# A Perceiver layer with a mixture of experts: the experts' first product with the weight's blocks held in TensorE and the 128 tokens streamed

## The reference

```python
x = x + xattn(layernorm(x), ctx, bias, mask)     # 2048 context rows per batch
x = x + attn(layernorm(x))
x = x + ffn(layernorm(x), gate_w, w1, w2)

def ffn(x, gate_w, w1, w2):                       # 8 experts, hidden width 2048
    k = int(2.0 * t / 8)                          # 32 tokens per batch and expert
    probs = softmax(x @ gate_w).transpose(0, 2, 1)
    g, m = top_k(probs, k)
    xin = gather(x, m)                            # 4 x 32 = 128 tokens per expert
    h = gelu(einsum('nekd,edf->nekf', xin, w1))   # 128 x 512 by 512 x 2048
    h = einsum('nekf,efd->nekd', h, w2)           # 128 x 2048 by 2048 x 512
    return scatter_add(g[..., None] * h, m).astype(bfloat16)
```

## Time and profile before

| | us |
|---|---|
| median of 3 runs | 471.69 |
| the 3 runs | 471.41, 471.69, 473.98 |
| the profiled execution | 471.49 |
| its span in the trace | 469.8 |
| granted TensorE clock, mean over the span | 0.995 |

### The profile page before, as it was taken

The page is one execution under the profiler, slowest core; times in us unless marked ns, Lnnn a source line. Parts: engine busy times, 40 slices in busy tenths (PEclk is TensorE's granted clock), DMA queues, the critical chain, the costliest instruction groups (busy, mean ns, idle before and its releaser), DMA issues.

```text
span 469.8 us, 9797 instructions
## 1 busy us (share of the span) xinstructions
PE 438.9 (93%) x3401; PEld 365.7 (78%) x3401; DVE 370.8 (79%) x515; ACT 296.4 (63%) x614; POOL 82.1 (17%) x93
## 2 busy tenths in 40 slices
PE   0989999999998999989997999999999999999994
PEld 0968888888887779878875877887878787878794
DVE  5986777777777886748887999898989898898862
ACT  1535666666665752566422877777787878777852
POOL 5000000000000014000013250503223140505002
PEclk9998999999999999999999999999999999999999
DMA  7792000000000462430000099999999989898002
GB/s 265 254 340 69 25 23 23 23 23 23 23 23 1 176 229 91 161 108 3 1 1 1 3 374 387 387 387 387 379 341 331 361 309 372 292 383 299 16 1 89
DMA packets 43537, 82.02 MB, mean 175 GB/s; under 512 B 3064, under 2 KB 4216, under 8 KB 43512
## 3 DMA queue, kind: packets, MB, share of 16 engines
q1 hardware_dynamic: 39320, 75.85, 45.2%
q10 hardware_dynamic: 4192, 5.83, 3.7%
HBM read 80.58 MB, written 1.10 MB: 174 GB/s over the span
## 4 chain that ended last, share of the span: by engine, by line
PE 72%; DVE 12%; ACT 8%; DMA 3%; issue 2%; POOL 0%; DVEq 0%; SPq 0%; ACTq 0%
PE po L1526 18%; PE pk L1526 11%; PE pv L1526 10%; PE pv L1202 6%; ACT big_a L455 6%; PE ps L1218 5%; PE ps L1280 3%; PE pv L1218 3%; PE po L1552 3%; DVE mc L839 3%; PE ps L1273 2%; PE po L1301 1%; DMA rows<-kb 1%; PE pk L1218 1%; PE po L1218 1%
## 5 line engine op out<-in xcount | busy, mean ns | idle before, releaser
L1137 DVE TENSOR_TENSOR w_lo<-att_w,w_hi 128x2048 fp32r<-128x2048 f32 x60 | 137.9, 2306 | 21.6 <-ACT w_hi L649 21.6
L649 ACT CAST w_hi<-att_w 128x2048 fp32r<-128x2048 f32 x60 | 114.9, 1915 | 15.6 <-PE po L1526 15.6
L455 ACT ACTIVATE big_a<-ps,negm 128x128 f32<-128x128 f32 x176 | 62.3, 407 | 21.0 <-DVE negm L842 21.0
L1526 PE MATMUL po<-w_hi,ht_hi 128*128 128x512 f32 (+1 forms) x128 | 50.4, 393 | 0.0
L1526 PE MATMUL po<-w_hi,ht_lo 128*128 128x512 f32 (+1 forms) x128 | 48.7, 381 | 0.0
L1526 PE MATMUL po<-w_lo,ht_hi 128*128 128x512 f32 (+1 forms) x128 | 48.5, 379 | 0.0
L455 ACT ACTIVATION_READ_ACCUMULATOR big_a<-ps,negm 128x1 f32 x176 | 43.5, 247 | 0.0
L1192 PE MATMUL pk<-ctx_s,att_w 128*128 128x128 f32 x352 | 43.1, 282 | 0.0
L1192 PEld LDWEIGHTS pk<-ctx_s,att_w 128*128 128x128 f32 x352 | 41.4, 196 | 1.9 <-issue 1.8
L839 DVE TENSOR_REDUCE mc<-ps 128x8 f32<-128x1024 f32 x22 | 26.9, 1221 | 12.4 <-PE ps L1273 12.4
L390 POOL COPY q_now<-qk 128x512 f32 x10 | 6.9, 685 | 123.2 <-PE ps L1273 123.2
(11 more groups left out here) (315 smaller groups left out, 1017.3 us busy)
## 6 DMA issues: line engine op xcount, KB each, us to landing
att_w<-in_w SPq DMA_DIRECT2D x64, 1024.0 KB, 7.1
ctx_s<-in_ctx_t SPq DMA_DIRECT2D x11, 256.0 KB, 2.7
x_s<-in_x SPq DMA_DIRECT2D x4, 256.0 KB, 3.9
att_w<-in_wq SPq DMA_DIRECT2D x1, 1024.0 KB, 8.3
att_w<-in_wk SPq DMA_DIRECT2D x1, 1024.0 KB, 10.6
att_w<-in_wv SPq DMA_DIRECT2D x1, 1024.0 KB, 6.7
att_w<-in_sv ACTq DMA_DIRECT2D x1, 1024.0 KB, 7.6
att_w<-in_wo ACTq DMA_DIRECT2D x1, 1024.0 KB, 9.7
```

The lines of the kernel that those rows point to most:

```text
L455: ins = a.activation(big_a[:, h], ps[:, c, g * P:(g + 1) * P], ACT.Exp, bias=negm[:, h:h + 1], accum_out=sums[:, h:h + 1])
L649: a.copy(w_hi[:, i % SLOTS], att_w[:, i]).then_inc(hi_ok, 1)
L1137: v.tensor_tensor(w_lo[:, i % SLOTS], att_w[:, i], w_hi[:, i % SLOTS], ALU.subtract).then_inc(lo_ok, 1)
L1526: ins = mm(dst, l, r, start=start and i == 0, stop=i == len(terms) - 1, skip_group_check=True)
```

## The change

In hidden, the operands change places: the weight's 128 x 128 blocks are held and the 128 tokens streamed. For each of the 4 blocks of hidden columns and each of the 4 blocks of the contraction there are three matmuls of 128 columns, 48 per quarter. The output in pk or pv then has the hidden width on the partitions. The turns are dropped; gelu writes the same to h_s, and the high and low parts are made from h_s, no longer from a bank. gelu waits for the low part that read its half of h_s before, where it waited for the turn. hidden waits for the gelu that read its bank, now in all experts but the first from its first quarter on. The scatter stands behind hidden 2, no longer behind turn 0. On DVE the low part of the activations stands ahead of the low part of the weight tile.

```diff
@@ -206,7 +206,7 @@
         hi_ok = sem("hi_ok"); lo_ok = sem("lo_ok")
         tile_mm = sem("tile_mm")
         x_now_ok = sem("x_now_ok"); xin_hi_ok = sem("xin_hi_ok"); xin_staged = sem("xin_staged"); back_staged = sem("back_staged")
-        gelu_ok = sem("gelu_ok"); ht_mm = sem("ht_mm"); ht_hi_ok = sem("ht_hi_ok"); ht_lo_ok = sem("ht_lo_ok")
+        gelu_ok = sem("gelu_ok"); ht_hi_ok = sem("ht_hi_ok"); ht_lo_ok = sem("ht_lo_ok")
         y_ok = sem("y_ok"); y_hi_ok = sem("y_hi_ok"); y_lo_ok = sem("y_lo_ok"); sc_mm = sem("sc_mm")
         rounded_ok = sem("rounded_ok"); summed_up = sem("summed_up"); res_ok = sem("res_ok"); res_pool = sem("res_pool"); stored = sem("stored")
 
@@ -651,26 +651,18 @@
             def gelu(e, q):
                 act.wait_ge(tile_mm, e * 8 + (q + 1))
                 if q >= 2 or not isinstance(e, int):
-                    act.wait_ge(ht_mm, e * 4 + (q - 1))
+                    act.wait_ge(ht_lo_ok, e * 4 + (q - 1))
                 a.activation(h_s[:, q % 2], (pk, pv)[q % 2][:], ACT.Gelu_apprx_tanh).then_inc(gelu_ok, 1)
 
-            def transposed_hi(e, q):
-                act.wait_ge(ht_mm, e * 4 + (q + 1))
-                a.copy(ht_hi[:, q * 4:q * 4 + 4].rearrange("p c n -> p (c n)"), po[:, 1]).then_inc(ht_hi_ok, 1)
+            def high_part(e, q):
+                act.wait_ge(gelu_ok, e * 4 + (q + 1))
+                a.copy(ht_hi[:, q * 4:q * 4 + 4].rearrange("p c n -> p (c n)"), h_s[:, q % 2]).then_inc(ht_hi_ok, 1)
 
             def expert(e, more):
-                gelu(e, 0)
-                split_hi(e, 4)
-                gelu(e, 1)
-                transposed_hi(e, 0)
-                split_hi(e, 5)
-                gelu(e, 2)
-                transposed_hi(e, 1)
-                split_hi(e, 6)
-                gelu(e, 3)
-                transposed_hi(e, 2)
-                split_hi(e, 7)
-                transposed_hi(e, 3)
+                for q in range(NQ):
+                    gelu(e, q)
+                    high_part(e, q)
+                    split_hi(e, NQ + q)
                 if not more:
                     return
                 for i in range(SLOTS):
@@ -1136,16 +1128,16 @@
                 dve.wait_ge(hi_ok, e * 8 + (i + 1))
                 v.tensor_tensor(w_lo[:, i % SLOTS], att_w[:, i], w_hi[:, i % SLOTS], ALU.subtract).then_inc(lo_ok, 1)
 
-            def transposed_lo(e, q):
+            def low_part(e, q):
                 dve.wait_ge(ht_hi_ok, e * 4 + (q + 1))
                 part = slice(q * 4, q * 4 + 4)
-                v.tensor_tensor(ht_lo[:, part].rearrange("p c n -> p (c n)"), po[:, 1],
+                v.tensor_tensor(ht_lo[:, part].rearrange("p c n -> p (c n)"), h_s[:, q % 2],
                                 ht_hi[:, part].rearrange("p c n -> p (c n)"), ALU.subtract).then_inc(ht_lo_ok, 1)
 
             def expert(e, more):
                 for q in range(NQ):
+                    low_part(e, q)
                     split_lo(e, NQ + q)
-                    transposed_lo(e, q)
                 if not more:
                     return
                 for i in range(SLOTS - 1):
@@ -1537,25 +1529,23 @@
                 if isinstance(e, int) and e == 0:
                     pe.wait_ge(xin_dve, 2)
                 pe.wait_ge(lo_ok, (2, 3, 3, 4)[q] if isinstance(e, int) and e == 0 else e * 8 + (q + 1))
-                if q >= 2 or not isinstance(e, int):
+                if q >= 2 or not isinstance(e, int) or e > 0:
                     pe.wait_ge(gelu_ok, e * 4 + (q - 1))
-                passes((pk, pv)[q % 2][:], xin_hi, xin_lo, q % SLOTS, 0, True).then_inc(tile_mm, 1)
-
-            def turn(e, q):
-
-                pe.wait_ge(gelu_ok, e * 4 + (q + 1))
-                if isinstance(e, int) and e == 0 and q == 0:
-                    pe.wait_ge(xin_act, 6)
-                if q or not isinstance(e, int):
-                    pe.wait_ge(ht_lo_ok, e * 4 + q)
-                for c in range(KC):
-                    ins = nc.tensor.transpose(po[:, 1, c * P:(c + 1) * P], h_s[:, q % 2, c * P:(c + 1) * P], ident[:])
-                ins.then_inc(ht_mm, 1)
+                dst = (pk, pv)[q % 2]
+                for n in range(KC):
+                    at = slice(n * P, (n + 1) * P)
+                    for k in range(KC):
+                        for w, r in ((w_hi, xin_hi), (w_lo, xin_hi), (w_hi, xin_lo)):
+                            ins = mm(dst[:, at], w[:, q % SLOTS, k, at], r[:, k], start=k == 0 and w is w_hi and r is xin_hi,
+                                     stop=k == KC - 1 and r is xin_lo, skip_group_check=True)
+                ins.then_inc(tile_mm, 1)
 
             def expert_out(e, q):
 
                 pe.wait_ge(lo_ok, e * 8 + (NQ + q + 1))
                 pe.wait_ge(ht_lo_ok, e * 4 + (q + 1))
+                if q == 0 and isinstance(e, int) and e == 0:
+                    pe.wait_ge(xin_act, 6)
                 if q == 0 and not isinstance(e, int):
                     pe.wait_ge(y_ok, e)
                 passes(po[:, 0], ht_hi, ht_lo, q % SLOTS, q * KC, q == 0).then_inc(tile_mm, 1)
@@ -1586,6 +1576,8 @@
                 e = E - 1
                 pe.wait_ge(lo_ok, e * 8 + (NQ + q + 1))
                 pe.wait_ge(ht_lo_ok, e * 4 + (q + 1))
+                if half == 1 and q == 0:
+                    pe.wait_ge(gelu_ok, e * 4 + 3)
                 ins = passes((po[:, 0], pk)[half][:, 0:HALF], ht_hi, ht_lo, q % SLOTS, q * KC, q == 0,
                              slice(half * HALF, (half + 1) * HALF))
                 if q == NQ - 1:
@@ -1594,15 +1586,11 @@
             def last_expert(e, before):
                 hidden(e, 0)
                 hidden(e, 1)
-                turn(e, 0)
+                hidden(e, 2)
                 scatter(before)
-                hidden(e, 2)
-                turn(e, 1)
                 hidden(e, 3)
-                turn(e, 2)
                 last_out(0, 0)
                 last_out(1, 0)
-                turn(e, 3)
                 for q in range(1, NQ):
                     last_out(0, q)
                 last_out(1, 1)
@@ -1614,16 +1602,11 @@
             def expert(e, before):
                 hidden(e, 0)
                 hidden(e, 1)
-                turn(e, 0)
+                hidden(e, 2)
                 if before is not None:
                     scatter(before)
-                hidden(e, 2)
-                turn(e, 1)
                 hidden(e, 3)
-                turn(e, 2)
-                expert_out(e, 0)
-                turn(e, 3)
-                for q in range(1, NQ):
+                for q in range(NQ):
                     expert_out(e, q)
 
             expert(0, None)
```

## The result

| | before | changed | ratio, 95% interval |
|---|---|---|---|
| median of 4 runs, us | 471.55 | 538.62 | 1.142 [1.138, 1.147] |
| lowest to highest | 471.35 to 473.98 | 536.62 to 539.37 | |
| span of the profiled execution | 469.8 | 537.3 | |
| granted clock, mean | 0.995 | 0.995 | |

What follows compares the result with a forecast made beforehand. PE was taken to bound the expert stage. Eight experts at +10.30 us for loads and -1.76 for turns, less a 0.6 us stall, gave +67.7 on 471.5: 539 us, range 530 to 556.

Steps and rivals of the forecast that it cites:

- What bounds: Expert stage: every us of PE work is a us of the kernel; DVE, ACT, GpSimd and DMA work is covered.
- Part 2: First product: 48 matmuls of 128 columns at 0.112 us, set by weight loads; +2.58 us per quarter, +82.4 in all.
- the 492 us: First product at the skill's 81 ns per 128-column matmul: +20 us for the kernel; the prediction didn't trust it.
- Part 1: Expert stage: dropping 4 turns of 0.44 us gains 1.76 us per expert, 14.1 us in all, on PE.
- Part 3: High and low parts from h_s on ACT and DVE: same instructions, costed at nothing, covered by PE's 5.4 us quarter.
- Part 4: Last expert, second product's last quarter: its inputs are ready with 0.36 us to spare, so PE doesn't stall.
- A: First product: loads are quick, the stream sets 0.063 us; -7.5 us, 464 us; chance 0.05 for all paces below 0.109.
- B: First product: each narrow matmul makes two records like plain float; 238 us longer, 710 us; chance 0.06.
- D: An overlooked wait (a tile, a bank) adds some us more; 540 to 560 us; chance 0.03.
- C: Clock halves in narrow quarters, free there, costing 1.6 us per expert at the second product's start; 552 us; chance 0.06.

## Why the prediction was right, point by point

- **What bounds (PE alone).** Right. 8 x 8.45 - 0.6 gives 67.0 of the 67.5 us.
- **Part 2, the load.** Right: 0.112 was taken, and the quarters show 0.1106 to 0.1135 per matmul, 5.38 on average, as in the sum. That it is the load, then an inference from the earlier trace rows, is shown by the run with 64 columns held (0.060) and by the counts of loads: 48 take 5.38 us, 32 take 3.60. The difference from 512 to 256 columns in the earlier trace rows was no guide to 128 while the load stays as it is. The Trainium skill's 81 ns (TensorE: Matmul & The Clock Gate, Back-to-back issue gap) is refuted for this type, 111 measured, and with it the 492 us.
- **Part 1, the turns.** Right: 1.76 us per expert taken, 1.73 measured alone. The added 0.09 isn't peculiar to a turn: in the run without turns the quarters ahead of and behind the scatter take 2.90 us in place of 2.80 too, all of it in the step next to the scatter. These two steps were in the scatter's 0.87 already (0.67 + 2 x 0.10), so the sum was not hurt.
- **Part 3, ACT and DVE for nothing.** Right here, by its cover: DVE has 11 us of slack per expert. The sizes alone weren't the whole of it. Without the cover the low part from h_s grows beside GpSimd's work, at 3 us for the kernel.
- **Part 4, the last expert.** Right. DVE ended the last split at 521.52 + 2.29 = 523.81, and PE began its last quarter at 524.03, 0.22 us later, where I had 0.36.
- **Rivals.** A fell twice: by the pace here, and in that its condition, a quick load, gives 458 us when the block has 64 columns (464 was worked out with 0.063, 0.060 was measured). B fell: one record each. D did not occur: PE has no wait there. **C** did not occur, but its price was wrong. Its sentence "in the narrow quarters a half clock costs nothing" took the load to be independent of the clock. It nearly doubles there, and with 64 tokens the second product lost 2.66 us per expert, not 1.6. With 64 and 96 tokens the fall cost some 140 us and gave 678 to 680, not 13 and 552, and my range would have missed it. Its reason against the fall, that PE is never idle there, was no protection either: in both runs the clock fell in a PE that never waited. Its other reason, the full clock at the gate, rests on 8 narrow matmuls in 0.89 us. So it was partly luck that the clock held: with a quarter fewer tokens it fell.

## What to carry to other kernels

Before narrow streams are put in the place of wide ones, count the weight loads: at the full clock a product costs here about the larger of its loads x 0.111 us and its columns' stream, so 29 loads were the break-even against 12 wide matmuls and a turn, and the change made 48. Price a turn that way too: a turn's 4 transposes, 0.44 us together, are cheap beside 36 added loads. And before calling the half clock harmless, read the load records at either clock; a stage made of loads took nearly twice as long there.

## What was not expected of the hardware

- **Fewer tokens, half the clock.** 128 columns per load: granted clock 1.00 in the experts' stretches. 96 and 64: 0.50 for most of each expert, and 678 to 680 us in place of 539. PE was busy all the time in both.
- **The load goes with TensorE's clock and with width and type.** 0.111 us at full clock and 0.213 at half for 128 columns of 4 bytes, at most 0.060 for 64 columns at full clock. The 2-byte load has a record half as long.
- **GpSimd beside DVE.** With both inputs in SBUF, DVE's low part took up to 1.80 us instead of 0.69. It works the other way as well. GpSimd's xin_lo, in the kernel before and in the changed one:

```profile
L420 POOL TENSOR_TENSOR xin_lo<-x_now,xin_hi x7: 3268/3280/3314, 278.0 to 428.1; 128x512 fp32r<-128x512 f32 x7
```

```profile
L420 POOL TENSOR_TENSOR xin_lo<-x_now,xin_hi x7: 1729/1733/1741, 285.7 to 486.4; 128x512 fp32r<-128x512 f32 x7
```

  The same subtraction took 3.28 us and 1.73 us. The difference is what DVE had begun just before: there a w_lo of 2.29 us, here a low part of 0.69. The subtraction ended 1.16 us after that DVE instruction in both (306.35 after 305.19, and 320.88 after 319.72), and in the run without turns too (324.87 after 323.71). So it seems to wait for all of the DVE instruction. The run with the staging cut shows this most plainly, where GpSimd had only 8 columns to copy:

```profile
319.42 2.29 DVE L1129 TENSOR_TENSOR w_lo<-att_w,w_hi 128x2048 fp32r<-128x2048 f32 x1
```

```profile
319.74 2.03 POOL L417 COPY x_now<-qk 128x8 f32 x1 [0.84 <-PE pv L1518]
```

  The copy lasts until 321.77, w_lo until 321.71, and in the other six experts the copy ends with a w_lo as well. The Trainium skill (SBUF — State Buffer, Who interferes with whom) says that a DVE instruction with two inputs in SBUF contends with a GpSimd instruction that reads SBUF; the runs agree, 0.69 against 1.80 us. Of DVE in its 2-port modes it also says that whoever issues first has the shared pair of ports for the whole instruction and the other is blocked; these runs show such a wait for subtractions with two inputs in SBUF too, of which it says only that they contend. It fits the other way round: the w_lo that began at 321.02 beside a GpSimd cast that ended at 321.57 was 0.40 us longer than the usual 2.29.
